# A two-layer attention kernel: the fourth value tile of batches 1 to 7 moved ahead of the first score tile

## The reference

```
q = einsum('bcn,dc->bnd', x, Wq) + bq
k = einsum('bcn,dc->bdn', ctx, Wk) + bk[:, None]
v = einsum('bcn,dc->bdn', ctx, Wv) + bv[:, None]
attn = softmax(einsum('bnd,bdm->bnm', q, k), axis=2)
x = einsum('bcm,bnm->bcn', v, attn) + x          # first layer

theta, phi, g = 1x1 convolutions (512 to 256) of x, ctx, ctx
W = theta^T phi / 1024
y = W g^T                                        # second layer, linear
out = batchnorm(w_w y + w_b) + x
```

## Time and profile before

| | us |
|---|---|
| median of 3 runs | 1126.97 |
| lowest, highest run | 1123.3, 1127.23 |
| span of the profiled execution, first to last instruction | 1122.5 |
| TensorE busy in it | 1061.0 |
| VectorE busy in it | 708.3 |
| ScalarE busy in it | 468.6 |
| GpSimd busy in it | 298.7 |

### The profile page before, as it was taken

How to read it: one execution, slowest core, us unless ns; L and a number is a source line. 1 busy time by engine, 2 the same in 40 slices (tenths; PEclk the granted TensorE clock), 3 DMA queues, 4 the chain that set the end, 5 groups by cost and what they waited for, 6 DMA issues and landing times.

```text
span 1122.5 us, 13860 instructions
## 1 busy us (share of the span) xinstructions
PE 1061.0 (95%) x5144; PEld 889.3 (79%) x5144; DVE 708.3 (63%) x905; ACT 468.6 (42%) x802; POOL 298.7 (27%) x198
## 2 busy tenths in 40 slices
PE   5999999999799998999989999899998999989998
PEld 4788878887688876888768887688876888768886
DVE  6884377735777357673577726777277663777635
ACT  7653444425334253343534335443354433544231
POOL 0311252123421234112351134401344013440130
PEclk9999999999999999999999999999999999999999
DMA  8335241351414514145142442324423244232412
GB/s 276 102 81 174 78 172 39 101 181 57 151 38 108 174 57 151 40 116 164 61 146 51 113 156 72 136 54 113 152 76 132 59 113 148 76 131 66 116 45 75
DMA packets 80626, 122.05 MB, mean 109 GB/s; under 512 B 13104, under 2 KB 46384, under 8 KB 80560
## 3 DMA queue, kind: packets, MB, share of 16 engines
q1 hardware_dynamic: 80560, 121.17, 35.0%
HBM read 70.79 MB, written 16.78 MB: 78 GB/s over the span
## 4 chain that ended last, share of the span: by engine, by line
PE 72%; DVE 11%; DMA 7%; issue 5%; ACT 3%; POOL 1%; SPq 0%; DVEq 0%; ACTq 0%
PE pG L545 31%; PE pG L464 11%; PE pG L455 10%; DMA out_dram<-xr 6%; PE pG L556 6%; DVE xr L857 4%; PE pG L484 4%; DVE xr L852 3%; PE pM L524 2%; PE pM L533 2%; PE pS L495 2%; DVE qs L756 1%; PE pT L497 1%; PE pT L495 1%; PE pS L497 1%
## 5 line engine op out<-in xcount | busy, mean ns | idle before, releaser
L545 PE MATMUL pG<-pt,vT 128*128 128x512 f32 x1536 | 352.6, 390 | 0.3 <-DVE pt L807 0.3
L545 PEld LDWEIGHTS pG<-pt,vT 128*128 128x128 f32 x1536 | 287.3, 188 | 59.4 <-issue 0.5
L886 POOL TENSOR_TENSOR xms<-xr,xms 128x512 fp32r<-128x512 f32 x64 | 94.2, 1487 | 338.0 <-ACT xms L693 338.0
L455 PE MATMUL pG<-wv,x2s 128*128 128x512 f32 x768 | 179.8, 391 | 0.7 <-DVE wv L715 0.7
L455 PEld LDWEIGHTS pG<-wv,x2s 128*128 128x128 f32 x768 | 143.0, 188 | 30.3 <-DVE wv L715 1.1
L836 DVE SCALAR_TENSOR_TENSOR xr<-pG,cl,xr 128x512 f32<-128x512 f32 x64 | 48.0, 750 | 164.2 <-PE pG L545 163.5
L464 PE MATMUL pG<-x2Ts 128*128 128x256 f32 (+2 forms) x768 | 129.8, 327 | 0.0
L464 PEld LDWEIGHTS pG<-x2Ts 128*128 128x128 f32 x768 | 119.2, 192 | 9.5
L878 POOL TENSOR_TENSOR x2Ts<-x2T_f,x2Ts 128x512 fp32r<-128x512 f32 x64 | 91.0, 1450 | 122.8 <-ACT x2Ts L640 122.8
L807 DVE TENSOR_TENSOR pt<-mv,pt 128x512 fp32r<-128x512 f32 x128 | 80.9, 688 | 47.2 <-ACT pt L670 47.2
L882 POOL TENSOR_TENSOR ys<-yf,ys 128x256 fp32r<-128x256 f32 x32 | 31.2, 975 | 285.0 <-ACT ys L661 285.0
(11 more groups left out here) (102 smaller groups left out, 1307.3 us busy)
## 6 DMA issues: line engine op xcount, KB each, us to landing
mv<-tp SPq DMA_DIRECT2D x512, 64.0 KB, 2.0
st<-in_ctx_dram SPq DMA_DIRECT2D x32, 512.0 KB, 6.2
st<-in_x_dram SPq DMA_DIRECT2D x32, 512.0 KB, 4.4
x2T_f<-in_ctx2T_dram SPq DMA_DIRECT2D x32, 512.0 KB, 5.8
xr<-in_x_dram SPq DMA_DIRECT2D x64, 256.0 KB, 3.5
out_dram<-xr SPq DMA_DIRECT2D x64, 256.0 KB, 2.5
wv_f<-in_wvT_dram SPq DMA_DIRECT2D x4, 256.0 KB, 7.7
wpg_f<-in_wpgT_dram SPq DMA_DIRECT2D x1, 1024.0 KB, 6.0
```

The source lines that it names most:

```text
L455: last = mm(bank, x2s[:, l, c, 128 * m:128 * m + 128], wv[:, r, c, :], start=(c == 0 and n == 0), stop=(c == 3 and n == 2))
L545: last = mm(bank, vT[:, l, m, 128 * c:128 * c + 128], pt(h)[:, r, m, :], start=(m == 0 and n == 0), stop=(m == 7 and n == 2))
L886: done(tt(xms(h)[:, c, LO, :], xr[c][:, :], xms(h)[:, c, HI, :].bitcast(F), ALU.subtract), "xlo")
```

## The change

For batches 1 to 7 the fourth value tile, `v:3`, is taken out of its place behind the four Gram tiles (ahead of `S:4`) and put ahead of `gs` and `S:0`, behind `v:2`. Its two evictions move too: on ScalarE from behind the exponential of `S:3` to between the copies `x2T:6` and `x2T:7`, and on VectorE from behind `G:3` to behind `v:2`, ahead of the maximum of `S:0`. `V_FIRST` goes from 3 to 4 for these batches: `v:3` now has number 3 instead of 7, and the Gram tiles have 4 to 7 instead of 3 to 6. The tiles `v:4` to `v:7` keep 8 to 11. Batch 0, SyncE and GpSimd are as before, and no instruction is added or taken away.

```
-V_FIRST = (5, 3)
+V_FIRST = (5, 4)
...
 LATER = dict(
     pe=(
-        "k:0 q:0 q:1 k:1 v:0 v:1 v:2 gs S:0 S:1 G:0 S:2 S:3 G:1 G:2 gt G:3 v:3 S:4 S:5 GT:0 GT:1 v:4 v:5 v:6 "
+        "k:0 q:0 q:1 k:1 v:0 v:1 v:2 v:3 gs S:0 S:1 G:0 S:2 S:3 G:1 G:2 gt G:3 S:4 S:5 GT:0 GT:1 v:4 v:5 v:6 "
...
     act=(
-        "q s x2T:0 x2T:1 k v:0 k2 q2 x2T:2 x2T:3 x2T:4 x2T:5 v:1 v:2 x2T:6 x2T:7 gs S:0 S:1 G:0 S:2 G:1 gt "
-        "G:2 G:3 S:3 v:3 T:0 T:1 v:4 GT:0 GT:1 S:4 v:5 v:6 S:5 v:7 T:2 T:3 Y:0 Y:1 Y:2 S:6 Y:3 S:7 mts T:4 "
+        "q s x2T:0 x2T:1 k v:0 k2 q2 x2T:2 x2T:3 x2T:4 x2T:5 v:1 v:2 x2T:6 v:3 x2T:7 gs S:0 S:1 G:0 S:2 G:1 gt "
+        "G:2 G:3 S:3 T:0 T:1 v:4 GT:0 GT:1 S:4 v:5 v:6 S:5 v:7 T:2 T:3 Y:0 Y:1 Y:2 S:6 Y:3 S:7 mts T:4 "
...
     dve=(
-        "s q k v:0 k2 q2 v:1 v:2 S:0 S:1 n:0 tr:0 S:2 G:0 n:1 tr:1 G:1 S:3 G:2 n:2 tr:2 n:3 tr:3 G:3 v:3 T:0 "
+        "s q k v:0 k2 q2 v:1 v:2 v:3 S:0 S:1 n:0 tr:0 S:2 G:0 n:1 tr:1 G:1 S:3 G:2 n:2 tr:2 n:3 tr:3 G:3 T:0 "
```

## The result

The changed kernel takes 1153.06 us in the median of four runs (1150.39 to 1154.24), the kernel before 1127.1 (1123.3 to 1127.95, four runs). The ratio is 1.0224, with a 95% interval of 1.02 to 1.0249: **slower by 26 us**. The forecast was 1149 with a range of 1140 to 1157.

The account below looks back on a forecast made before the run. TensorE was taken to bound the kernel (72% of the chain, busy 1061.0 of 1122.5 us). 7 x (0.71 + 0.93 + 1.0) = 18.5, plus 4 for the clock, 22.5 on the median 1126.97: 1149; range 1140 to 1157.

Parts of the forecast that it names:

- bank of `v:3`: Ahead of `v:3`: it must wait until `v:1` is read out of `pG1`, closing the gap 0.71 us later a batch.
- the wait at `S:5`: Without `v:3` ahead of `S:4`, `S:5` waits for the exponential of `S:3`: 1.0 us a batch, bounds 0.85 to 1.3.
- `gs` uncovered: `gs`, now between `v:3` and `S:0`, leaves TensorE's waiting time and adds 0.93 us a batch, at most 1.09.
- clock, net: Low clock behind all seven gaps instead of four, 1.6 us each time: 4 us in all, bounds 0 and 6.
- upper terms: High end: 7 x (0.75 + 1.09 + 1.3) plus 6 gives 1155; 0.4 a batch behind it adds 2.8, 1158.
- The gap is not filled: Ahead of `S:0`: `v:3` fills none of TensorE's gap, its bank not being free; new gaps 3.91 to 5.59 us.
- The first rival: `v:3` fills the gap ahead of `S:0`: about 1115.7 us, 6 lower if the clock stayed up; chance 0.03.
- VectorE's lead: At `v:7` and `PV`: VectorE's lead about used up, taken as 0, bounds 0 to 0.4 us a batch.
- a deduction for the part inside the gap: Low-clock time inside the longer gap costs nothing, so three more times 1.6, 4.8 us, was taken as 4.

## Why the prediction was right

The sum by term, from ratios against the kernel before (1% is 11.3 us), with the run that shows each:

| term | forecast | measured | from |
|---|---|---|---|
| bank of `v:3`, and the wait at `S:5` | 12.0 | 11.7 | 1.0032 less 0.9928 |
| `gs` uncovered | 6.5 | 6.3 | 1.0088 less 1.0032 |
| clock, net | 4 | 7.2 | 15.3 (1.0224 less 1.0088) less 8.1 (0.9928) |
| sum | 22.5 | 25.2 | 1.0224 |

The ratios have intervals of 0.15 to 0.3% to either side, so the last term is good to some 4 us; the rows below narrow it. The first line of the table holds two waits that no pair of runs took apart; their split, 0.63 and 1.04 a batch, comes from the rows. The prediction's own upper terms add up to 1158, and its range ends at 1157; nothing hangs on it.

**The gap is not filled: right.** `v:3` names line 760 as its releaser in all seven batches, 0.78 us behind `q2` in each, against the 0.86 that the forecast put there (0.71 more than the 0.15 of `S:0`). The gaps are 3.50 to 5.40, forecast as 3.91 to 5.59. They grew by 0.91 to 1.71 a batch, not by 1.64 each, because the gap itself moves with the output transfers: `k2` (line 613) names them as its releaser in all seven, and in each the growth is 1.56 (0.63 and 0.93) plus what that wait changed by, -0.66 to +0.15, within 0.02. The run with the bank set free shows that this one wait decides between 2.2% slower and 1.3% faster. The first rival had set 1115.7 for a bank free in time, and 6 less if the clock stayed up; that run measured 1111.35. The Trainium skill's rotation rule (*Perfetto Trace Analysis*, section *Matmuls*), by which `v:3` would have filled the gap, holds in the run with the early eviction, where `v:3` waits for no bank, and not in the changed kernel, where it waits 3.50 to 5.40 us.

**gs on the path: right**, 6.3 to 6.4 measured for 6.5.

**The wait at S:5: right in size, wrong in cause.** 1.04 us by rows for 1.0. But the prediction gave it to ScalarE's order, left VectorE's chain to the upper bound, and said it did not depend on the other terms. The row of the transpose at 625.29 and the run with the exponential first show two limits 0.25 us apart, ScalarE's copy of `G:3` and VectorE's chain of scaling and transposing. Removing the wait locally gave 0.1 us with low clocks and 1.2 without.

**VectorE's lead: right as a risk, taken as zero.** The forecast said the lead at `v:7` and `PV` would be used up. In the changed kernel `v:4` to `PV` takes 18.57 us (628.40 to 646.97) against 18.58 before, and 18.57 to 18.64 in all seven: nothing is lost there. That the wait at `S:5` had just given VectorE part of its lead back is the likely reason, argued and not shown by itself; where that wait was taken out, waits came up at `v:6`, and in some batches at `PV`.

**The clock: right mechanism, mis-sized.** All seven gaps brought the low level, as forecast. The failed step is the price, carried over as 1.6 us a time from the kernel before, with a deduction for the part inside the gap. By rows: from the end of `q2` to the start of `v:4` the kernel before took 24.69 (batches 4 and 7) or 24.75 (1) at full clock and 26.26 to 26.28 in the four others. The changed kernel took 30.01, 29.69, 29.93, 28.61, 29.46, 28.74 and 29.39. At full clock it would be 24.69 plus 0.63 (bank, 0.78 less 0.15), 0.93 and 1.04, so 27.29. The rest is 1.3 to 2.7 a batch, 14.8 in all, against 6.4 before: **8.4 net, not 4**. The filled kernels bear the working out: this stretch takes 27.31 to 27.35 in all seven batches with the fifteen filling matmuls, 26.33 to 26.35 with `gs` ahead of the filling, and 24.66 to 24.74 in the kernel before with its eight. In five batches the low clock lasted twice as long as any before, which no row of the kernel before showed. The deduction went the wrong way: part of the low stretch did fall into the gap, but in those five more followed.

One thing in the rows separates the two lengths, and it is not the gap: behind 4.15 us the low level lasted 3.4, behind 3.75 it lasted 6.8. The four 3.4 us stretches of the kernel before began when TensorE had been back at work for 0.37 to 1.28 us. In the changed kernel the fall came while it was still idle: for another 0.35 and 0.58 us in batches 6 and 4, where the low level lasted 3.4, and for 0.94 to 2.27 in the other five. The traces of the four other kernels here whose clock fell in these batches agree: in all 37 stretches, 3.4 us where TensorE was back no later than 0.58 us after the fall (17 times), 6.8 where it came back 0.67 us or more after it (20 times). No run set this on purpose, so it is a regularity of these traces and not a cause shown.

By the same rows this stretch of the seven batches takes 205.8 us where it took 179.2, 26.6 more. The span grew by 26.1, so all of the loss lies there, and the rest is as before but for half a microsecond in all. That rest holds a low stretch of 3.4 us in batch 0 (from 36.8), which the trace of before has not; up to its `PV` batch 0 took 0.7 us more, and no instruction of it had changed.

## What to carry to other kernels

Before moving work into an engine's idle time, ask what that work itself must wait for, buffers included, and where the release stands in the queue of the engine that gives it: here it stood behind the very instruction that ended the gap. Count also what the moved work pushes out of the gap (`gs`) and what it covered where it stood (`S:5`), and try the missing eviction's move together with it, since each half alone made this kernel slower. On TensorE idle time has a second price in the clock, and it is not proportional: a slow stretch lasted 3.4 or 6.8 us here, and the longer ones came where TensorE was still idle for some time after the clock had fallen.

## What the runs showed of the hardware

Not expected: the low level lasted 6.8 us behind five gaps of 3.75 to 5.40 us, with TensorE at work without a break for the last 5 to 6 of it in batch 1, while behind the four gaps of the kernel before where it came (2.59 to 3.95) it lasted 3.4. In six traces the length went with the idle time left after the fall (at most 0.58 us, or 0.67 and more), not with the length of the gap. And 56 matmuls whose result nobody reads made the kernel before 0.7% faster (0.9928), by keeping the clock at its 2.4 GHz level.
